# Masking of the attention weights moved between engines: one minimum on VectorE for heads 0 to 2, TensorE for head 3, GpSimd none

## The reference

```
q, k, v  = heads of (norm(x) @ wq.T + bq), (ctx @ wk.T + bk), (ctx @ wv.T + bv)   # 16 heads of 16
scores   = q @ k.T / 4
scores   = where(mask == 0, -1e9, scores)          # one mask (512, 512) for all batches and heads
x        = x + (softmax(scores) @ v) @ wo.T + bo
y        = square(relu(norm(x) @ W_fc.T)) @ W_proj.T
mem = 0; repeat 5 times: mem = 0.9 * mem + y - (mem > 1);  spikes += mem > 1
x        = x + spikes / 5
```

## Time and profile before

| | |
|---|---|
| median of 3 runs | 2750.03 us (2748.4 to 2750.82) |
| the profiled execution's own time | 2749.74 us |
| its span | 2747.9 us |
| TensorE busy | 2615.5 us, 95% |
| VectorE busy | 2192.6 us, 80% |
| ScalarE busy | 1744.1 us, 63% |
| GpSimd busy | 1759.3 us, 64% |
| granted TensorE clock, mean | 0.983 |

### The profile page before, as it was taken

The page is one execution under the profiler, slowest core; times in us unless marked ns, Lnnn a source line. Parts: engine busy times, 40 slices in busy tenths (PEclk is TensorE's granted clock), DMA queues, the critical chain, the costliest instruction groups (busy, mean ns, idle before and its releaser), DMA issues. The chain is left out here.

```text
span 2747.9 us, 55326 instructions
## 1 busy us (share of the span) xinstructions
PE 2615.5 (95%) x19045; PEld 1784.4 (65%) x19078; DVE 2192.6 (80%) x3270; ACT 1744.1 (63%) x2871; POOL 1759.3 (64%) x998
## 2 busy tenths in 40 slices
PE   6999999999999999999998879999999999999996
PEld 3877777777877777777887754545454545454523
DVE  5999999999999999999998949494848485858573
ACT  5878877877887788788778433545444444444342
POOL 3999999999999999999999814232323232323130
PEclk9999999999999999999999999999999999999978
DMA  3122212212221221112122061404040404040300
GB/s 123 51 78 67 89 42 79 89 44 78 74 82 41 80 82 64 65 66 100 33 78 102 9 192 46 123 2 122 2 122 2 122 2 122 2 122 2 107 2 16
DMA packets 102090, 187.08 MB, mean 68 GB/s; under 512 B 14720, under 2 KB 75264, under 8 KB 100256
## 3 DMA queue, kind: packets, MB, share of 16 engines
q1 hardware_dynamic: 101840, 183.92, 21.3%
HBM read 148.38 MB, written 35.52 MB: 67 GB/s over the span
## 5 line engine op out<-in xcount | busy, mean ns | idle before, releaser
L983 DVE TENSOR_TENSOR_SCAN h<-dA,pair 128x512 f32<-128x512 f32 x1024 | 1172.8, 1202 | 103.1 <-PE pair L476 91.8
L1122 POOL TENSOR_TENSOR hC<-h,C_rep 128x1024 f32<-128x1024 f32 x512 | 1200.2, 2368 | 74.0 <-DVE h L983 66.4
L720 ACT ACTIVATE dA<-delta,cols 128x511 f32<-128x511 f32 x1024 | 664.3, 711 | 32.2 <-DVE h L983 26.1
L476 PE MATMUL pair<-diagB,duT 64*128 64x128 f32 x8192 | 549.0, 281 | 25.0 <-DVE h L983 15.8
L476 PEld LDWEIGHTS pair<-diagB,duT 64*128 64x128 f32 x8192 | 485.9, 188 | 127.2 <-issue 96.6
L577 PE MATMUL y_bank<-ident,hC 128*128 128x128 f32 x3980 | 523.7, 277 | 11.9 <-POOL hC L1122 10.1
L577 PEld LDWEIGHTS y_bank<-ident,hC 128*128 128x128 f32 x3980 | 442.3, 141 | 104.4 <-issue 50.9
L1903 DVE CUSTOM_DVE_ANT_0 masked<-pair,mask_bias 128x512 f32<-128x512 f32 x512 | 321.9, 687 | 19.7 <-PE pair L1382 13.5
L1635 ACT ACTIVATE pr<-pair 128x1024 f32<-128x1024 f32 x256 | 248.3, 1021 | 74.9 <-PE pair L1382 74.9
L2007 POOL CAST m_part<-m_rest 8x512 bf16<-8x512 f32 x16 | 9.6, 603 | 414.8 <-ACT m_rest L1635 414.8
L476 PE MATMUL general<-xnT,w_in 128*128 128x512 f32 x496 | 241.8, 602 | 4.5 <-ACT xnT L720 3.5
(11 more groups left out here) (186 smaller groups left out, 3239.2 us busy)
## 6 DMA issues: line engine op xcount, KB each, us to landing
C_rep<-c_rows SPq DMA_DIRECT2D x128, 512.0 KB, 4.2
qk_parts<-qk_part SPq DMA_DIRECT2D x96, 256.0 KB, 4.1
w_in<-w_in SPq DMA_DIRECT2D x16, 1024.0 KB, 4.8
k_st<-qk_parts SPq DMA_DIRECT2D x8, 1536.0 KB, 9.1
q_st<-qk_parts SPq DMA_DIRECT2D x8, 1536.0 KB, 9.4
x_in<-x SPq DMA_DIRECT2D x18, 512.0 KB, 4.1
w_out<-w_out SPq DMA_DIRECT2D x17, 512.0 KB, 4.3
mid<-x_out SPq DMA_DIRECT2D x9, 512.0 KB, 4.8
```

The lines of the kernel that those rows point to most:

```text
L476: return pe.matmul(o, lhsT, rhs, start=start, stop=stop)
L720: return act.activation(o, i, fn, **kw)
L983: last = dve.tensor_tensor_scan(h[:, g % 4, i, :], dA[:, g % 4, i, :], dBu[:, i, :], 0.0, ALU.mult, ALU.add)
L1122: last = pool.tensor_tensor(hC[:, g % RING], h[:, g % 4], C_rep[:, 2 * j:2 * j + 2, :], ALU.mult)
```

## The change

ON_POOL and GpSimd's `mask_exp` go, with keep_word and its VectorE setup. In units 1 to 7, tile t = 1, heads 0, 1 and 2 are no longer masked in PSUM. VectorE's new `keep_exp(b, unit)` waits for the exponential of head 2 and computes min(exp, mask_bias + 2^32) in place over the three heads in one instruction of 128x1536 elements. Head 3 is masked by TensorE. `weigh(u, 1)` waits for VectorE's semaphore instead of GpSimd's. The seven calls of `keep_exp` stand among the spike passes, for which `step` can be issued in parts (0: tmp, 1: mem, 2: cnt).

```diff
-ON_POOL = ((1,), (3,))
+ON_DVE = (0, 1, 2)
...
-    keep_word = sb("keep_word", [P, 2, T], i32)
...
-                        on_pool = unit > 0 and t == 1 and hh in ON_POOL[half]
-                        last = mm(pair[hh % 2][:, t, :], k_st[0:QR, hd, kt * P:(kt + 1) * P], q_st[0:QR, hd, :], True, on_pool)
-                        if not on_pool:
+                        kept_later = unit > 0 and t == 1 and hh in ON_DVE
+                        last = mm(pair[hh % 2][:, t, :], k_st[0:QR, hd, kt * P:(kt + 1) * P], q_st[0:QR, hd, :], True, kept_later)
+                        if not kept_later:
                             last = mm(pair[hh % 2][:, t, :], ident_bf[:, :], mask_biasT[:, kt, :], False, True)
...
-                    pe.wait_ge(s_kept.sem, s_kept.count(b * (H - 2) + unit * 2 - 1))
+                    pe.wait_ge(s_kept_dve.sem, s_kept_dve.count(b * (H // 2 - 1) + unit - 1))
...
-            dve.tensor_scalar(keep_word[:, :, :], mask_biasT[:, 1::2, :], 0.0, None, ALU.is_equal).then_inc(s_word.sem, 1)
...
+            def keep_exp(b, unit):
+
+                kt = 2 * (unit % 2) + 1
+                dve.wait_ge(s_exp.sem, s_exp.count(b * 2 * H + unit * 4 + ON_DVE[-1]))
+                exps = pr[:, ON_DVE[0]:ON_DVE[-1] + 1, kt, :]
+                dve.scalar_tensor_tensor(exps, mask_biasT[:, kt, :].unsqueeze(1).broadcast_to((P, len(ON_DVE), T)), -MASKED, exps,
+                                         ALU.add, ALU.min).then_inc(s_kept_dve.sem, 1)
...
                 step(1)
+                keep_exp(b, 1)
                 if more:
                     norm_apply(ATT, b + 1, x1n, xn_q)
-                step(2)
+                step(2, (0,))
+                keep_exp(b, 2)
+                step(2, (1, 2))
                 if isinstance(it, int):
                     dve.wait_ge(early.mid.sem, early.mid.count(B))
+                keep_exp(b, 3)
                 normalise(0, it)
-                step(3)
+                step(3, (0,))
+                keep_exp(b, 4)
+                step(3, (1, 2))
+                keep_exp(b, 5)
                 normalise(1, it)
-                step(4)
+                step(4, (0,))
+                keep_exp(b, 6)
+                step(4, (1, 2))
+                keep_exp(b, 7)
                 finish()
                 normalise(2, it)
                 normalise(3, it)
...
-                for unit in range(1, H // 2):
-                    for half in range(2):
-                        mask_exp(b, unit, half)
```

More of the change, by code:

```diff
@@ L1269, in attention_pass @@
     s_exp = stage("exp", ahead=2)
-    s_kept = stage("masked_exp")
-    s_word = stage("mask_words")
+    s_kept_dve = stage("masked_exp_dve")
     g_out = stage("g_out")
@@ L1821, in start, with step @@
                         dve.tensor_scalar(cnt[c], y_sb[c], THRESHOLD, None, ALU.is_gt)
-                def step(i):
+                def step(i, parts=(0, 1, 2)):
                     for c in cols_of:
-                        dve.drain()
-                        if i == 1:
-                            dve.scalar_tensor_tensor(tmp[c], y_sb[c], BETA, y_sb[c], ALU.mult, ALU.add)
+                        if 0 in parts:
                             dve.drain()
-                            dve.scalar_tensor_tensor(mem[c], y_sb[c], THRESHOLD, tmp[c], ALU.is_gt, ALU.subtract)
-                        else:
-                            dve.scalar_tensor_tensor(tmp[c], mem[c], -BETA, y_sb[c], ALU.mult, ALU.add)
-                            dve.drain()
-                            dve.scalar_tensor_tensor(mem[c], mem[c], -THRESHOLD, tmp[c], ALU.is_lt, ALU.subtract)
-                        dve.drain()
-                        dve.scalar_tensor_tensor(cnt[c], mem[c], -THRESHOLD, cnt[c], ALU.is_lt, ALU.add)
+                            if i == 1:
+                                dve.scalar_tensor_tensor(tmp[c], y_sb[c], BETA, y_sb[c], ALU.mult, ALU.add)
+                            else:
+                                dve.scalar_tensor_tensor(tmp[c], mem[c], -BETA, y_sb[c], ALU.mult, ALU.add)
+                        if 1 in parts:
+                            dve.drain()
+                            if i == 1:
+                                dve.scalar_tensor_tensor(mem[c], y_sb[c], THRESHOLD, tmp[c], ALU.is_gt, ALU.subtract)
+                            else:
+                                dve.scalar_tensor_tensor(mem[c], mem[c], -THRESHOLD, tmp[c], ALU.is_lt, ALU.subtract)
+                        if 2 in parts:
+                            dve.drain()
+                            dve.scalar_tensor_tensor(cnt[c], mem[c], -THRESHOLD, cnt[c], ALU.is_lt, ALU.add)
                 def finish():
@@ L2021, in _ @@
             take_x1(0)
[L2023 to L2033, removed]
             def batch(b, more):
```

## The result

The changed kernel takes 2733.59 us (median of five, 2732.32 to 2737.02) against 2750.41 for the kernel before in the same comparison: ratio 0.9942, 95% interval 0.9929 to 0.9956, so 16 us or 0.6% faster. The profiled execution took 2733.53 us, 16.2 less than the one profiled before. A later comparison gave 2733.60 against 2749.98 (0.9941, 0.9928 to 0.9955).

The account below looks back on a forecast made before the run. TensorE was taken to bound the weights stretch end to end. Gains of 10.6 + 4.3 less 1.5 gave 13.4 us off 2749.74, and 0.3 more to stand beside the median: 2736.6 us, range 2732 to 2744.

Parts of the forecast that it names:

- Term A: Weights stretch: masks taken off TensorE save 6 x 0.22 = 1.32 us an item, 10.6 us in all; unit 1 saves nothing.
- Term B: End of the weights stretch: weigh(7, 1) can start at S + 3.99 instead of S + 4.53, 0.54 us an item, 4.3 in all.
- Term C: Units 1 to 6: weigh(u, 1) now waits for VectorE's minimum, which is there in time; cost 0.
- Term D: With GpSimd's 112 masks gone, nearly all VectorE spike passes take 1.23 us and the minimum 1.76; none on the path itself.
- Term E: Later store of tmp holds k(0) by 1.35 us, within slack; only the first item's 4.6 us landing costs, -1.5 us.
- The handovers: Rival, chance 0.13: ScalarE's handovers eat half of the gain from masks taken off TensorE, giving 2741.4 us.
- the store holds k(0): Rival, chance 0.11: tmp's store holds k(0) in every item; 2745.6 us with 4.6 us landings everywhere, 2740 with half.
- VectorE's slow passes: Rival, chance 0.04: slow passes not GpSimd's doing, minimum takes 3.2 us, VectorE bounds unit 7; 28 us lost, 2778.

Follow-up runs that it names:

- experiment that leaves A out: The changed kernel, but TensorE masks head 0 of the second key tile again, 400 mask matmuls as before; 2746.66 us.
- four-head kernel: The changed kernel, but in units 1 to 6 VectorE masks all four heads of the second key tile in one minimum; 2729.91 us.
- three heads on GpSimd: The kernel before, but GpSimd masks heads 0 to 2 of the second key tile in one multiplication, TensorE head 3; 2764.74 us.
- late finish: The changed kernel with finish moved behind normalise(2); 2742.07 us.
- finish first: The changed kernel with finish ahead of the minimum of unit 7 instead of behind it; 2739.78 us.

## Why the prediction was right, step by step

**Direction and size.** 2736.6 was forecast, 2733.6 measured, inside the range. 13.4 us were forecast and 16.2 measured between the profiled executions. In the steps:

**Term A** (six masks an item, 1.32 us) was right: 1.32, shown by putting one mask back. Unit 1 indeed saves nothing, or it would be 1.54. ScalarE did not become the bound: in the last halves it still waits 0.47 us for TensorE ahead of its pair of exponentials.

**Term B** (0.54 us at the end) was a little too big: 0.48 in the experiment that leaves A out. The step that failed is the start of weigh(7, 0) at S + 2.99. I derived it from the exponentials and forgot TensorE's own queue: seven matmuls, a weigh and the four transposes of `to_tokens`, 1.63 + 1.00 + 0.58 = 3.21 us, stand ahead of it, and it starts at 2000.14 = S + 3.21, as before. The 0.32 us that weigh(7, 1) had waited for GpSimd is gone, and about 0.13 more comes from the two weighs following without a gap (`project_k` 1.86 us behind weigh(7, 0), not 1.99). In single matmuls, which the row above merges, weigh(7, 1) starts 0.88 us behind weigh(7, 0), not the 1.00 that I took from a weigh with scores behind it. So the forecast put weigh(7, 0) 0.22 us too early and weigh(7, 1) 0.12 us too far behind it; the two errors work against each other, and that B comes within 0.06 is in part luck. The minimum was sized right, 1.76 us, and ended at S + 3.68 where S + 3.69 was forecast.

**Term C** (no wait in units 1 to 6) was right: the matmuls never wait for VectorE's pr, and only 8 weight loads do, one an item, ahead of time (us in total, times, the longest):

```profile
PEld y_bank L1380 <- DVE pr L1903: 2.9, 8, 0.4
```

The four-head kernel shows how near the queue is to mattering.

**Term D** was right: of the 88 passes of 1024 columns that write tmp from mem or cnt, mem from tmp, and cnt from mem, 41 took over 1.3 us before, and one does now. An item's opening passes, which stand beside GpSimd's work on the maxima, still take up to 2.02 us. That B and C hold because of D is argued, not shown: no run has minima on VectorE beside a busy GpSimd. In the strict form of the Trainium skill's rule ("SBUF — State Buffer", who interferes with whom) a pass that starts under a GpSimd mask waits for its whole end; with three heads on GpSimd the pass at 2002.21 did so within 0.15 us.

**Term E** was right in place and in slack (0.3 us by the late finish), and wrong in its one cost: -1.5 us for the first item's store. Its landing of 4.6 us is not there in the changed kernel, where the slowest of the ten takes 3.0:

```profile
DMA to landing us min/median/max: 2.1/2.9/3.0
```

The first item's store takes 3.0 us in all nine profiles with minima on VectorE, and 3.5 in the other kernel with masks on GpSimd (three heads). I had carried a landing over from one kernel to another; what made it long is not shown. This is the largest single term of the miss of 2.8 us. Terms that no edit explains give another 2.4: 0.9 us ahead of the first raw score, 0.7 in the first item, and about 0.8 at the last item's start. Against them stand 0.5 that B lacked and the 0.5 that the first stretches lose (last section). What can be put down to the change is so 8 x 1.80 - 0.5 = 13.9 us; that 13.4 was forecast is near it because a cost that did not come, 1.5, stands against 1.0 of gain that did not come either, which is luck. As for the last item's start, TensorE's granted clock came up later there in the profile before (windows, the column behind the engines' busy times is the clock):

```profile
2640.00:2642.00 2.00, 2.00 (x7) 0.60 (x5) 1.93 (x2) 1.32 (x2) 1.87 (x2) 0.50 0.00 0
```

and here in the profile after, as far behind the transposes of the maxima:

```profile
2626.00:2628.00 2.00, 2.00 (x8) 0.56 (x6) 1.93 (x2) 1.91 (x2) 1.87 (x2) 0.93 0.00 0
```

The rivals did not come true. The handovers took nothing from A; the store holds k(0) but not k(1); and VectorE's slow passes went with GpSimd's masks, and were back, at up to 4.3 us, where GpSimd had masks in one piece.

## What to carry to other kernels

Work taken off the bounding engine counts instruction by instruction, but only if the engine that takes it is on time at the one place where nothing covers it, here the last unit: put the short job there and keep the queue ahead of it empty. Where a pass with slack is moved behind one on the path, follow its consumers through to the DMA and the buffer that waits for it. And when a stretch repeats to 0.01 us, measure stretches: between finish first and the changed kernel, some 2 us of cause stood beside 4 that no edit explains.

## What was not expected of the hardware

The tail of the program differs in length. From the last item's first `on` transpose to the end of the span, it takes 60.9 us before, 61.0 in the changed kernel, and 64.6 with finish first, whose code there is the same. Over the eleven profiles it is 60.7 to 61.0 in six, 62.9 in one (four heads) and 64.4 to 64.7 in four. The windows behind that transpose show it, first of the changed kernel, then with finish first (start:end, length, busy times, then the granted clock):

```profile
2670.70:2680.70 10.00, 4.81 (x24) 3.81 (x24) 3.85 (x12) 1.08 (x2) 1.26 (x2) 1.00 0.01 3
2680.70:2690.70 10.00, 8.35 (x19) 4.41 (x20) 0.91 (x3) 3.30 (x6) 0.00 (x0) 0.66 0.00 0
```

```profile
2674.00:2684.00 10.00, 7.75 (x24) 5.78 (x24) 2.88 (x6) 1.17 (x2) 0.00 (x0) 0.66 0.00 0
2684.00:2694.00 10.00, 5.50 (x12) 3.06 (x13) 1.88 (x9) 1.19 (x2) 1.26 (x2) 0.55 0.00 1
```

The same 24 matmuls take 7.75 us of TensorE at a mean clock of 0.66 instead of 4.81 at 1.00: with finish first the clock falls to its lower level, 1.2 GHz, within the first two microseconds of this thinly filled stretch, comes back some 6 us later, and falls again about 11 us behind the start; in the changed kernel it falls once, about 10 us behind the start. What decides it is not shown, nor whether it goes with the program or with the single execution: the changed kernel alone was profiled twice, with 61.0 us both times. It puts 3.6 us into a comparison of kernels that differ by 2.

All programs with minima on VectorE also lose 0.09 us in each first stretch (43.53 against 43.44), where no instruction was changed; the one with three heads on GpSimd does not. In an item compared instruction by instruction the loss is there 14 us behind the first raw score and does not grow after that. The cause is open.
